# Layer 3's edge passes: the weighing one turn later, PE's work in halves, and five output banks between the passes

## What is computed

```python
k = (x @ Wk).reshape(n, H, D)
q = (x @ Wq).reshape(n, H, D)
v = (x @ Wv).reshape(n, H, D)
k_e, q_e, v_e = (k[src], q[dst], v[src])
is0 = (etype == 0)[:, None, None]
kw = jnp.where(is0, einsum('ehd,hdf->ehf', k_e, Watt[:, 0]), einsum('ehd,hdf->ehf', k_e, Watt[:, 1]))
m  = jnp.where(is0, einsum('ehd,hdf->ehf', v_e, Wmsg[:, 0]), einsum('ehd,hdf->ehf', v_e, Wmsg[:, 1]))
a = (kw * q_e).sum(-1) * pri[:, etype].T / np.float32(np.sqrt(D))
amax = jax.ops.segment_max(a, dst, num_segments=n)
ea = jnp.exp(a - amax[dst])
att = ea / jax.ops.segment_sum(ea, dst, num_segments=n)[dst]
h = jax.ops.segment_sum(m * att[:, :, None], dst, num_segments=n).reshape(n, H * D)
h = h @ Wa
alpha = jax.nn.sigmoid(skip)
return h * alpha + x * (1.0 - alpha)
```

## Time and profile before

| | |
|---|---|
| median of 3 runs | 7328.54 us (7322.5 to 7334.62) |
| the profiled execution, time | 7332.78 us |
| its span | 7330.6 us |
| PE, DVE, ACT, POOL busy over the span | 69%, 64%, 40%, 48% |
| first edge pass of layer 3 | about 4888 to 5625 us |
| the stage between the passes (`renew`) | about 5703 to 5909 us |
| second edge pass | about 5909 to 6641 us |

### The profile page before, as it was taken

How to read it: one execution, slowest core, us unless ns; L and a number is a source line. 1 busy time by engine, 2 the same in 40 slices (tenths; PEclk the granted TensorE clock), 3 DMA queues, 4 the chain that set the end, 5 groups by cost and what they waited for, 6 DMA issues and landing times. The chain is left out here.

```text
span 7330.6 us, 108212 instructions
## 1 busy us (share of the span) xinstructions
PE 5055.0 (69%) x21503; PEld 3608.8 (49%) x21504; DVE 4711.4 (64%) x11833; ACT 2945.6 (40%) x7221; POOL 3519.8 (48%) x3532
## 2 busy tenths in 40 slices
PE   4763777767765967769666667777776767776764
PEld 4763444444444834558544457644444444444453
DVE  6876577667775168550566662379997379995453
ACT  2552355455544220022223332237775157773331
POOL 1776377447730267731167703336663056660014
PEclk9999977777777988979877778999999999997887
DMA  3442344334423943339334417756664167761036
GB/s 89 165 140 69 97 128 128 69 104 127 127 58 112 310 110 101 103 75 334 115 96 107 106 39 257 243 166 212 211 210 122 50 181 212 211 210 45 18 120 197
DMA packets 523817, 1021.67 MB, mean 139 GB/s; under 512 B 143645, under 2 KB 284498, under 8 KB 514846
## 3 DMA queue, kind: packets, MB, share of 16 engines
q0 software_dynamic: 191360, 489.21, 24.6%
q1 hardware_dynamic: 301663, 497.07, 21.0%
q10 hardware_dynamic: 30528, 32.52, 1.3%
HBM read 927.97 MB, written 90.27 MB: 139 GB/s over the span
## 5 line engine op out<-in xcount | busy, mean ns | idle before, releaser
L733 POOL DMA_INDIRECT l_hgt_ep_g<-l_tkm,l_hgt_ep_ix x832 | 922.4, 1109 | 441.3 <-PE l_hgt_ep_out L831 237.6
L744 POOL DMA_INDIRECT l_gat_ep_g<-l_gat_th,keep_e_src x832 | 863.4, 1038 | 439.8 <-issue 232.2
L831 PE MATMUL l_gat_ep_out<-l_gat_ep_g,l_gat_ep_here 128*126 128x264 f32 x1664 | 712.0, 570 | 137.4 <-DVE l_gat_acc L988 131.9
L831 PEld LDWEIGHTS l_gat_ep_out<-l_gat_ep_g,l_gat_ep_here 128*126 128x126 f32 x1664 | 387.8, 264 | 369.0 <-DVE l_gat_acc L988 301.7
L2495 DVE TENSOR_TENSOR f_moe_experts_yb<-f_moe_experts_py,f_moe_experts_b2s 128x256 f32<-128x256 f32 x208 | 88.4, 425 | 719.7 <-PE f_moe_experts_py L2478 700.7
L831 PE MATMUL l_hgt_ep_out<-l_hgt_ep_g,l_hgt_ep_here 128*126 128x288 f32 x1664 | 500.4, 424 | 53.8 <-DVE l_hgt_ep_g L974 52.3
L2446 POOL DMA_INDIRECT f_moe_experts_xg<-f_moe_tx,f_moe_tok x208 | 197.3, 949 | 708.2 <-PE f_moe_experts_px L2459 625.2
L872 ACT COPY l_gat_ep_stage<-l_gat_ep_out 30x264 f32<-30x264 f32 x832 | 306.3, 371 | 524.5 <-PE l_gat_ep_out L831 516.7
L2510 ACT ACTIVATE f_moe_experts_ht<-f_moe_experts_phid,f_moe_experts_b1b 128x128 f32<-128x128 f32 x848 | 241.3, 372 | 673.1 <-PE f_moe_experts_phid L2469 671.5
L525 POOL DMA_INDIRECT recs<-place_stage,place_pos x392 | 424.8, 1084 | 138.5 <-issue 117.1
L2831 POOL DMA_INDIRECT l_edges_g<-l_table,keep_e_src x416 | 412.3, 991 | 146.8 <-issue 119.8
(11 more groups left out here) (652 smaller groups left out, 11794.6 us busy)
## 6 DMA issues: line engine op xcount, KB each, us to landing
l_hgt_ep_hot<-locrow SPq DMA_DIRECT2D x208, 256.0 KB, 4.8
f_moe_experts_w1b<-in_L_ffn_w SPq DMA_DIRECT2D x32, 1024.0 KB
f_moe_experts_w2b<-in_L_ffn_w SPq DMA_DIRECT2D x32, 1024.0 KB
f_moe_experts_w1b<-in_L_ffn_w SPq DMA_DIRECT2D x64, 512.0 KB, 5.0
f_moe_experts_w2b<-in_L_ffn_w SPq DMA_DIRECT2D x64, 512.0 KB, 5.2
f_moe_experts_w1b<-in_L_ffn_W SPq DMA_DIRECT2D x56, 512.0 KB
f_moe_experts_w2b<-in_L_ffn_W SPq DMA_DIRECT2D x56, 512.0 KB
l_gat_ep_hot<-locrow SPq DMA_DIRECT2D x104, 256.0 KB
```

Of the source, the lines that this page charges most:

```text
L733: gp.indirect_dma_start(g[:, b % NB, j, 0:W], None, table, bass.IndirectOffsetOnAxis(ap=ix[:, b, j:j + 1].bitcast(U32), axis=0)).then_inc( ...
L744: gp.indirect_dma_start(g[:, k % NB, j, 0:W], None, table, bass.IndirectOffsetOnAxis(ap=idx[:, k * CT + j:k * CT + j + 1].bitcast(U32), ax ...
L831: pe.matmul(out[:, t % 4, 0:WO], here[:, b % 2, t, :], g[:, b, t, F:F + WO], start=True, stop=True).then_inc(s_out, 1)
```

## The change

In the pass: DVE's reduction becomes a step of its own (`by_head`); the weighing of turn k-1 follows it; then both scans of turn k; add(2) and add(3) of turn k-2; the subtraction; add(0) and add(1) of turn k-1. The adds' block numbers are loaded two at a time. PE's `queries` is split into halves of two tiles, and PE's list starts with total(1), now of turn k-3. ACT's list starts with take(1), now of turn k-4, and rows_here is of k-2. In `renew`, for the call between the passes: `pt0`, `out0` and `pt1` have one bank each, and `out1` is a ring of five banks used cut by cut; the first two cuts have semaphores of their own when they are ready (`s_cut`), and the first has one when DVE has copied it (`s_first`).

```diff
-            def queries(k, b):
-                blks = list(asked)
-                pe.wait_ge(s_hot, k + 1)
-                if later(k, 1):
-                    pe.wait_ge(s_prod, k)
-                for h in range(2):
+            def queries(h):
+                def body(k, b):
+                    if h == 0:
+                        pe.wait_ge(s_hot, k + 1)
+                        if later(k, 1):
+                            pe.wait_ge(s_prod, k)
                     for j in range(HT):
                         mm = pe.matmul(found[:, h, j * D:j * D + D], hot[0:P, b % 2, 128 * (h * HT + j):128 * (h * HT + j) + 128],
-                                       look[:, bass.ds(blks[h * HT + j], 1), :].rearrange("p o c -> p (o c)"), start=True, stop=True)
-                mm.then_inc(s_found, 1)
+                                       look[:, bass.ds(asked[h * HT + j], 1), :].rearrange("p o c -> p (o c)"), start=True, stop=True)
+                    if h == 1:
+                        mm.then_inc(s_found, 1)
+                return body
...
-                piped(pe, NCH, [(2, total(0)), (0, whose), (1, turn), (2, total(1)), (1, turn_back), (0, queries)], NB)
+                piped(pe, NCH, [(3, total(1)), (0, whose), (0, queries(0)), (1, turn), (2, total(0)), (1, turn_back), (0, queries(1))], NB)
...
-                piped(act, NCH, [(3, take(0)), (3, take(1)), (2, exponent), (0, one_hot), (1, rows_here)], NB)
+                piped(act, NCH, [(4, take(1)), (2, rows_here), (3, take(0)), (2, exponent), (0, one_hot)], NB)
...
-                    v.drain()
-                    v.tensor_reduce(r, g[:, b, :, 0:D].rearrange("p t (h d) -> p t h d", h=H), AX.X, ALU.add).then_inc(s_raw, 1)
+
+            def by_head(k, b):
+                v.drain()
+                v.tensor_reduce(raw[:, b % 2, :, :], g[:, b, :, 0:D].rearrange("p t (h d) -> p t h d", h=H), AX.X, ALU.add).then_inc(s_raw, 1)
...
-                    n = HT if kind != "hgt" else CT
-                    if t % n == 0:
-                        blks[t:t + n] = blocks_of(core, mybir.EngineType.DVE, k * CT + t, n)
+                    if t % HT == 0:
+                        blks[t:t + HT] = blocks_of(core, mybir.EngineType.DVE, k * CT + t, HT)
...
-                return (2 if t >= HT and kind != "hgt" else 1), body
+                return (2 if t >= HT else 1), body
...
-                piped(v, NCH, [now(score), add(0), now(scan), add(1), now(scan_back), add(2), now(less), add(3), now(weigh(0))], NB)
+                piped(v, NCH, [now(score), now(by_head), (1, weigh(0)), now(scan), now(scan_back), add(2), add(3), now(less), add(0), add(1)], NB)
...
-    B0, B1 = (1, 1) if part and wide else (2, 2)
+    shared = part is not None and wide
+    B0, B1 = 1 if shared else 2, 2
...
-            out0 = ph.psum("out0", [P, 2, 512])
+            out0 = ph.psum("out0", [P, B0, 512])
...
-            pt1 = ph.psum("pt1", [128, 2, 512])
-            out1 = ph.psum("out1", [P, B1, len(cuts), 512])
+            pt1 = ph.psum("pt1", [128, B0, 512])
+            out1 = ph.psum("out1", [P, 1, 5, 512] if shared else [P, B1, len(cuts), 512])
+            s_cut = [ph.sem(f"cut{n}") for n in range(2)] if shared else []
+            s_first = ph.sem("first") if shared else None
...
-                        if t >= B1:
+                        if t >= B1 and not shared:
                             pe.wait_ge(s_take, t - B1 + 1)
...
                         for n, (c, d) in enumerate(cuts):
+                            if shared and len(cuts) * t + n >= 5:
+                                before, cut = divmod(len(cuts) * t + n - 5, len(cuts))
+                                pe.wait_ge((s_first, s_half, s_take)[cut], before + 1)
...
-                    v.wait_ge(s_mm, t + 1)
+                    v.wait_ge(s_cut[0] if shared else s_mm, t + 1)
...
+                    if shared:
+                        o.then_inc(s_first, 1)
+                        v.wait_ge(s_mm, t + 1)
+                        o = v.tensor_copy(dst[:, t, :], made_in(t, 2, M - passing))
```

More of the change, by code:

```diff
@@ L1988, in _ @@
                         for n, (c, d) in enumerate(cuts):
+                            if shared and len(cuts) * t + n >= 5:
+                                before, cut = divmod(len(cuts) * t + n - 5, len(cuts))
+                                pe.wait_ge((s_first, s_half, s_take)[cut], before + 1)
                             for k in range(2):
-                                mm = pe.matmul(out1[:, t % B1, n, 0:d - c], xt_of(t)[:, k, :], w[:, k, c:d], start=k == 0, stop=k == 1)
+                                mm = pe.matmul(made_in(t, n, d - c), xt_of(t)[:, k, :], w[:, k, c:d], start=k == 0, stop=k == 1)
+                            if shared and n < 2:
+                                mm.then_inc(s_cut[n], 1)
                         mm.then_inc(s_mm, 1)
@@ L2019, in _ @@
                         act.wait_ge(s_mm, t - 1)
-                    act.copy(xt_of(t).rearrange("p k c -> p (k c)"), pt1[:, t % 2, 0:2 * P]).then_inc(s_xt, 1)
+                    act.copy(xt_of(t).rearrange("p k c -> p (k c)"), pt1[:, t % B0, 0:2 * P]).then_inc(s_xt, 1)
                 t = i - 6
                 if passing > 512 and t >= 0:
-                    act.wait_ge(s_mm, t + 1)
+                    act.wait_ge(s_cut[1] if shared else s_mm, t + 1)
                     if t >= 4:
                         act.wait_ge(s_store[t % 4], 32 * (t // 4))
-                    act.copy(rows[:, t % 4, 512:passing], out1[:, t % B1, 1, 0:passing - 512]).then_inc(s_half, 1)
+                    act.copy(rows[:, t % 4, 512:passing], made_in(t, 1, passing - 512)).then_inc(s_half, 1)
                 if twin and t >= 0:
@@ L2104, in _ @@
                         v.wait_ge(s_mm0, t + 1)
-                        o = v.scalar_tensor_tensor(out=x[:, t, :], in0=part["old"][:, t, :], scalar=part["rest"], in1=out0[:, t % 2, 0:D], op0=ALU.mult, op1=ALU.add)
+                        o = v.scalar_tensor_tensor(out=x[:, t, :], in0=part["old"][:, t, :], scalar=part["rest"], in1=out0[:, t % B0, 0:D], op0=ALU.mult, op1=ALU.add)
                         if back is not None:
@@ L2116, in _ @@
                         v.drain()
-                        v.tensor_tensor(x[:, t, :], x[:, t, :], out0[:, t % 2, 0:D], ALU.add).then_inc(s_x, 1)
+                        v.tensor_tensor(x[:, t, :], x[:, t, :], out0[:, t % B0, 0:D], ALU.add).then_inc(s_x, 1)
                         v.drain()
@@ L2144, in _ @@
                         else:
-                            v.tensor_copy(rows[:, t % 4, 0:min(passing, 512)], out1[:, t % B1, 0, 0:min(passing, 512)])
-                    if passing and not twin:
+                            o = v.tensor_copy(rows[:, t % 4, 0:min(passing, 512)], made_in(t, 0, min(passing, 512)))
+                    if shared:
+                        o.then_inc(s_first, 1)
+                        v.wait_ge(s_mm, t + 1)
+                        o = v.tensor_copy(dst[:, t, :], made_in(t, 2, M - passing))
+                    elif passing and not twin:
                         o = v.tensor_copy(dst[:, t, :], out1[:, t % B1, passing // 512, passing % 512:passing % 512 + M - passing])
```

14 lines of the change are left out of this document (8 added, 6 removed).

## The result

The changed kernel takes 7575.16 us in the median (7573.2 to 7580.6, 4 runs), the kernel before, on the same chip, 7330.1 us (7322.5 to 7334.6). The ratio is 1.0335, with a 95% interval of 1.0319 to 1.0352: 3.4% slower. The forecast was 7412 with a range to 7500. The direction was right, the size was not; the time lies outside the range.

The account below looks back on a forecast made before the run. DVE was taken to bound layer 3's two edge passes: turn 7.40 against 6.84 us, +116 over 208 turns, -34 for five banks, +2 for longer lag, +84 in all on 7328.5: 7412 us, range 7300 to 7500.

Parts of the forecast that it names:

- DVE sets the pace, the path of the turn: Layer 3's edge passes: DVE's eleven steps in the new order set the turn, 7.40 us against 6.84.
- the sum: DVE's step times over one turn of the edge passes, added up: 7.40 us, ends 6.38 and 7.75.
- Adds in pairs, 0.66 instead of 0.37: DVE, two pairs a turn: an add directly behind another waits 0.21 us idle, so 0.66 instead of 0.37.
- the rival that decided under 0.45 a pair: DVE's paired adds: the second starts at once, no semaphore cost; turn 6.82, 7292 us; chance 0.12.
- The load for add 2, 0.78: DVE, block numbers loaded behind the backward scan: exposed, 0.78 us from scan to add 2; lower end 0.34.
- The load for add 0, 0.25: DVE, block numbers loaded behind subtraction and references: mostly hidden, 0.25 us from references to add 0, range 0.20 to 0.50.
- PE's clock costs nothing, PE keeps 0.6 us in hand: PE in the passes: transpose back ends at 1.7 us, subtraction due at 2.3, so nothing waits for PE.
- The ring at 3.10 + L: Late copies, keep 1, row numbers' load, one-hot close within one turn: 3.10 us plus transfer L, expected 7.4, DVE still setting the forecast.
- Its rival: The one-hot's chain of waits binds the passes if L exceeds 4.30: turn 7.90, 7517 us; chance 0.22.
- The load hidden, 6.96: DVE: backward scan to add 2 stays 0.34, its load unexposed; turn 6.96, 7322 us; chance 0.12.
- both free, 6.38: DVE: neither the paired adds' wait nor the load is exposed; turn 6.38, 7201 us; chance 0.03.
- Five banks, -34 and an end at -36: Stage between the passes: PE's wide matmuls no longer wait for output banks, -34 us, ends 0 and -36.

Follow-up runs that it names:

- e10_keep_later: Changed kernel with one load of four block numbers behind the reduce and SyncE's second writing of carried rows one step later, against the kernel before: ratio 0.9978, 7314 us.

## Why the prediction failed, point by point

*DVE sets the pace, the path of the turn*: right. The eleven steps stand in the order and, but for two, with the durations of the sum.

*Adds in pairs, 0.66 instead of 0.37*: right, 0.67 with 0.21 us idle, in every pair of the time line. By the Trainium skill (VectorE: DVE Perf Modes, "The DRAIN you can't avoid") the semaphore costs nothing extra. These rows don't bear that out for a second add that takes its block number from a register, and the rival that decided under 0.45 a pair fell; a pair without the semaphore was not run. What the pairs cost as a whole is another matter: without them the turn was no shorter, in an order that exposed a load as well.

*The load for add 2, 0.78*: the mechanism was right, the size was not; 0.96 in the turn shown, 0.93 in the median. I took the load's duration from a row of loads of four numbers. The changed kernel loads two, and that takes 0.54.

*The load for add 0, 0.25*: **the step that failed**. I let it hide, as its issue "can run ahead under add 3". The issue does run ahead, but only until the load starts together with the subtraction, and subtraction and references are too short (0.28 and 0.17 us) to cover 0.54. From references to add 0 it measured 0.60, of which 0.44 idle. Even a load of 0.34 gives 0.37. My range for it ended at 0.50. Together the two load terms are 0.53 a turn in the turn shown, 110 us over 208 turns. In the low turns, where the load starts later, references to add 0 is 0.80, and over all turns it is 0.71 in the mean.

The floor of about 600 ns that the Trainium skill gives such a load (DMA: Bandwidth & Descriptors, "Latency and other measured facts") would have been nearer than the row I used. The rows have 0.34 for four numbers and 0.54 for two, both under that floor, but it pointed to the right side.

*PE's clock costs nothing, PE keeps 0.6 us in hand*: **wrong in the low turns**. The 0.6 us was worked out at 2.4 GHz. At 1.2 GHz four query products take 2.07 us and the margin is gone: the low turns are 0.47 longer than the others, 0.27 a turn in the mean, 57 us in all, of which about 0.12 a turn comes through the load for add 0. The fall of the clock was in no rival. With the loads hidden, the one-hot in time and the adds in pairs there are 24 or 11 low turns instead of 120; with the adds apart there are 89.

*The branch of the loop* had no term, though the change moved the multiply from behind the long weighing to behind a short add: 0.11 a turn over all turns. The base was off too: the mean turn of before is 6.91, 0.07 above the 6.84 that I started from.

The account of a mean turn: 7.40 in the sum, 0.50 to 0.53 for the loads, 0.11 branch, 0.27 clock, 8.28 in all against 6.91. That is 1.37 instead of 0.56, times 208 turns +285 instead of +116.

*The ring at 3.10 + L* (L is the time of the row numbers' transfer): right as a mechanism, and not binding here, since L is 3.7 in the median (I expected 4.3), which makes 6.8, and the turn has 7.9. Its rival gave 7517 for another reason than the one that came. Where the loads were hidden it bound at once, with L at 4.5.

*The load hidden, 6.96; both free, 6.38*: with both loads hidden the clear turn is 6.83, and references to add 0 is 0.10 and not 0.25, so the rest of the sum was sound.

*GpSimd and the gathers at nothing*: DVE waited for a gather 6.7 us in both passes, as before (6.0).

*Five banks, -34 and an end at -36*: -41. The 36.4 us of idle before the wide matmuls went to 0.0; the other 4.6 us of the stage I had not looked for.

*What would prove me wrong*: the pair's distance (0.67, not under 0.5) and L (3.7, not over 4.4) did not. Of the marks that I had named for a right forecast, the idle time before add 3 and add 1, that before add 2 (put down to issue) and the wide matmuls without idle time appeared. Turns of 7.4 us did not, and DVE did wait at the subtraction (22.1 us over 68 times) and at the multiply (17.4 us of issue over 46). The marks that appeared tested the mechanisms and not their sizes: the time was still 163 us off.

Still open is what takes PE's clock down in the changed kernel. In the kernel before, PE's longest regular wait was 1.24 us in the mean (for the reduce, 257.1 us over 207 times); in the changed kernel it is 1.84 (for the multiply, 361.5 us over 196). Six transposes there took the low turns from 117 to 97, twelve left 83 where the same chip had 122, and opening the ring of the one-hot took none away. But the kernel with the adds apart had 89 low turns almost without that wait. Whether a wait of DVE in one turn brings on the next low one was not tried.

## What to carry to other kernels

A register load on an engine's sequencer is an instruction with a duration of its own: put it behind a long instruction and not behind a few short ones, leave something between it and the instruction that needs it, and cost it by a row with the same count and alignment. When a change removes the waits of a turn, whatever they used to absorb becomes visible: the same second load cost 57 us where 0.5 us of other waits stood behind it, and by the 0.59 us a turn that it is exposed about 120 us (an estimate, 0.59 times 208) where they did not. And moving a step of one queue by one turn can shut a ring that took two: follow it through each queue, even if another bound hides it at first. The best kernel of these runs is the old passes with the five banks, 7290 us; the new order with the five banks, its one load hidden and its ring open, comes to 7301 (with overlapping intervals), so no variant of the new order gained anything over the old passes.

## What the runs showed of the hardware

The duration of a block numbers' load depends on what it fetches in a way I had not expected: four numbers from the start of a group of four 0.34 us, two numbers 0.54 (whether the first two or the last two of a group: 0.541 and 0.524 in the medians), and four that begin at the third of a group 0.97. The last is the line of the loads in e10_keep_later:

```profile
L667 DVEq TENSOR_LOAD <-keep_e_blk x99: 959/965/991, 4912.0 to 5595.8; - x99
```

Between the reduce and the weighing even the 0.97 costs nothing: from one to the other it is 1.14 us, as without a load. With an add there instead of the weighing it is 1.37. And PE's granted clock was 0.99 in passes with 6.9 us a turn and 0.85 with 8.3, a turn only a fifth longer, with the same matmuls in it.
